# Dealing the row stores of the last two batches over six expert blocks

## What is computed

```python
logits = jnp.einsum('bsd,de->bse', x, gate_w)
top_vals, top_idx = jax.lax.top_k(logits, K)              # K = 2 of E = 8
gate_scores = jax.nn.softmax(top_vals, axis=-1)
...
h = jax.nn.silu(x @ w1 + b1) * (x @ w2 + b2)              # for each expert, 128 -> 256
expert_out = h @ w3 + b3                                  # 256 -> 128
return jnp.einsum('ebsd,bse->bsd', expert_out, w_dense)
```

## Time and profile before

| | us |
|---|---|
| median of 3 runs | 1115.79 (1115.34 to 1119.27) |
| profiled execution, its span | 1191.7 |

### The profile page before, as it was taken

How to read it: one execution, slowest core, us unless ns; L and a number is a source line. 1 busy time by engine, 2 the same in 40 slices (tenths; PEclk the granted TensorE clock), 3 DMA queues, 4 the chain that set the end, 5 groups by cost and what they waited for, 6 DMA issues and landing times. The chain is left out here.

```text
span 1191.7 us, 19302 instructions
## 1 busy us (share of the span) xinstructions
PE 993.4 (83%) x5725; PEld 373.4 (31%) x5725; DVE 912.5 (77%) x1983; ACT 816.4 (69%) x1555; POOL 664.7 (56%) x1061
## 2 busy tenths in 40 slices
PE   4699979898998989989999898888888865888780
PEld 2122222222222222222232222222145643655550
DVE  6788889987989989998998978998635734444667
ACT  2138888887877888877887777888756743565640
POOL 3833045565675656856667565364346556566562
PEclk9999999998989999999998989999689978999995
DMA  8758766664556656565555654332322433343456
GB/s 202 143 127 250 151 154 159 133 132 142 109 152 126 133 137 125 155 130 123 147 117 151 118 128 116 87 99 72 110 60 85 159 121 107 110 131 116 136 175 229
DMA packets 369049, 159.63 MB, mean 134 GB/s; under 512 B 290656, under 2 KB 333552, under 8 KB 365232
## 3 DMA queue, kind: packets, MB, share of 16 engines
q1 hardware_dynamic: 347376, 122.06, 44.7%
q0 software_dynamic: 9088, 18.76, 4.6%
q10 hardware_dynamic: 12480, 17.57, 4.2%
HBM read 87.85 MB, written 71.82 MB: 134 GB/s over the span
## 5 line engine op out<-in xcount | busy, mean ns | idle before, releaser
L1246 DVE TENSOR_REDUCE neg_max<-bank 128x1 f32<-128x512 f32 x1024 | 643.1, 680 | 86.9 <-PE bank L1979 73.9
L1755 ACT ACTIVATE probs<-bank 128x512 f32<-128x512 f32 x1024 | 545.3, 605 | 119.4 <-PE bank L1991 91.9
L1979 PE MATMUL bank<-Kt,Qt 48*128 48x512 bf16 x1024 | 348.4, 405 | 72.1 <-DVE neg_max L1246 51.9
L1991 PE MATMUL bank<-Qt,Kt 51*128 51x512 bf16 x1024 | 344.4, 401 | 13.4 <-ACT probs L1755 11.7
L2004 PE MATMUL bank<-probs,Vt 128*16 128x512 f32 x2048 | 283.6, 627 | 0.0
L1137 POOL DMA_INDIRECT y_dram<-y_rows,row_in x156 | 153.4, 983 | 99.6 <-DVE y_rows L1646 57.7
L1979 PEld LDWEIGHTS bank<-Kt,Qt 48*128 48x128 bf16 x1024 | 75.4, 94 | 418.5 <-DVE neg_max L1246 345.8
L1062 POOL DMA_INDIRECT rows_dram<-rows,slot x128 | 127.0, 992 | 45.5 <-issue 32.6
L1883 ACT ACTIVATE probs<-bank,w3b_cur 128x512 f32<-128x512 f32 x78 | 52.8, 687 | 99.0 <-PE bank L2080 45.4
L1639 DVE SCALAR_TENSOR_TENSOR probs<-bank,w3b_cur,probs 128x512 f32<-128x512 f32 x78 | 58.2, 748 | 69.8 <-ACT probs L1883 54.4
L2078 PE MATMUL bank<-ht_first,w_cur 128*128 128x512 f32 x156 | 71.1, 456 | 40.5 <-ACT w_cur L1869 24.5
(11 more groups left out here) (234 smaller groups left out, 1228.0 us busy)
## 6 DMA issues: line engine op xcount, KB each, us to landing
o_dram<-o_sb ACTq DMA_DIRECT2D x64, 256.0 KB, 3.0
row_in<-rows_dram SPq DMA_DIRECT2D x39, 260.0 KB
Qt<-q_dram SPq DMA_DIRECT2D x64, 128.0 KB
Kt<-k_dram SPq DMA_DIRECT2D x64, 128.0 KB
y_in<-y_dram SPq DMA_DIRECT2D x16, 512.0 KB
q_dram<-q_parts SPq DMA_DIRECT2D x48, 128.0 KB, 4.8
k_dram<-k_parts SPq DMA_DIRECT2D x48, 128.0 KB, 5.5
rows_dram<-rows SPq DMA_DIRECT2D x4, 1040.0 KB, 5.7
```

The source lines that it names most:

```text
L1246: dve.tensor_reduce(neg_max[:, side, a, col:col + 1], score_a[m % 3][:], AX_X, ALU.max, negate=True).then_inc(s_max, 1)
L1755: act.activation(probs[:, 4 * (j % 2) + (k ^ 1)], score_b[n % 3][:], ACT.Exp).then_inc(s_exp, 1)
L1979: pe.matmul(score_a[m % 3][:], Qt[b % BUFS][first:first + ROWS, n, P * c:P * c + P], Kt[b % BUFS][first:first + ROWS, n], start=True, stop ...
L1991: pe.matmul(score_b[m % 3][:], Kt[b % BUFS][first:first + ROWS + PARTS, n, P * c:P * c + P], Qt[b % BUFS][first:first + ROWS + PARTS, n], ...
```

## The change

The eight row stores of batch 14 no longer stand ahead of the y stores of block 9. They are issued behind the y stores of blocks 9, 10 and 11, three, three and two. Those of batch 15 move likewise from ahead of the y stores of block 12 to behind those of blocks 12, 13 and 14. `front_slots` stays where it is, in pieces 9 and 12. The stores themselves, their order among each other (k = 0 first) and their semaphores are the same.

```diff
+            def scatter_tile(f, i):
+
+                k, t = i // TT, i % TT
+                pool.indirect_dma_start(rows_dram, bass.IndirectOffsetOnAxis(ap=slot[:, k, t:t + 1], axis=0),
+                                        rows[:, f % 2, k, t], None).then_inc(s_scattered[f % 2], DMA)
+
...
-                    9: lambda: (front_slots(NB - 2), scatter(NB - 2, 0), scatter(NB - 2, 1)),
-                    12: lambda: (front_slots(NB - 1), scatter(NB - 1, 0), scatter(NB - 1, 1)),
+                    9: lambda: front_slots(NB - 2), 12: lambda: front_slots(NB - 1),
                 }
...
             for n in range(N_BLOCKS):
                 piece(n)
                 scatter_y(n)
+                if 9 <= n < 9 + 6:
+                    f, part = NB - 2 + (n - 9) // 3, (n - 9) % 3
+                    for i in range(3 * part, min(3 * part + 3, 2 * TT)):
+                        scatter_tile(f, i)
```

## The result

The changed kernel takes 1128.72 us (median of 4 runs, 1123.37 to 1130.09), beside 1115.57 us (median of 4, 1106.44 to 1119.27) for the kernel before on the same chip. The ratio is 1.0114, interval 1.0086 to 1.0142: 12.7 us slower (9.6 to 15.8), where I had forecast 8.5 us. The plain medians differ by 13.2 us; I go by the ratio.

The account below looks back on a forecast made before the run. The end was taken to hang on when row_load(19) may issue, with POOL's indirect DMAs ahead of it. 0 for step 1 and 8.5 us for steps 2 and 3, on 1115.8, gave 1124.3 us; range 1112 to 1131.

Parts of the forecast that it names:

- Step 3: Batch 15's row stores end behind block 14's y stores, not ahead of block 12's: turn(19) 6.7 to 11.9 us later.
- Step 2: POOL waits for batch 14's last row store to land before writing batch 15's slots: 1.8 us, bounds 0 and 5.1.
- Step 1: Y stores of blocks 9 to 11 issue 10.1, 6.3 and 2.5 us earlier, which buys nothing: cost 0, gain 0.
- Was PE there in time to notice?: PE reaches turn(19) at about 987 us, ahead of 1003 old and 1015 new, so the whole difference shows.
- runs dry: POOL idles for some us behind block 15's y stores, since weigh(16) stands behind turn(19) on DVE.
- The rival of late signals: Unexplained waits after finished matmuls and stretched SP copies rule the timed runs too: 0 to +3.7 us, chance 0.22.
- The rival of a dissolved stall: Eight row stores in one run cause the expert stage's stall and dealing ends it: 7 us faster, chance 0.12.
- The rival of slow trips: PE trips of about 8 us make turn(19) late anyway and hide the moved wait: +2.0 us, chance 0.06.
- The idle copies: In the old kernel, SP's eight unstretched copies make turn(19) due at 20.8 us, against 21.7 through block 12's y stores.

Follow-up runs that it names:

- e0: The kernel before, unchanged, profiled a second time: span 1117.1 us, own time 1118.87 us.
- e3: The kernel before with batch 15's eight row stores moved as one run to behind block 12's y stores: 1116.83 us, ratio 1.0003.
- e2: The changed kernel with only batch 14's row stores dealt out, batch 15's at once ahead of block 12's y stores as before: 1118.02 us, ratio 1.0021.
- e6: The changed kernel, unchanged, run in the longer condition beside the kernel before: median 1189.87 us, ratio 0.9987.
- e5: The changed kernel with a second slot tile for batch 15, against the kernel before in the longer condition: ratio 0.9977.
- e1: The changed kernel with only batch 15's row stores dealt out, batch 14's at once ahead of block 9's y stores as before: 1124.66 us, ratio 1.0081.

## Why the prediction was right, point by point

**Step 3, the mechanism, holds within 2 us.** Measured from the end of y11:

| | forecast | measured |
|---|---|---|
| old: turn(19) behind y11 | 21.7 | 959.61 - 939.47 = 20.1 |
| new: turn(19) behind its own y11 | 33.6 + 2.5 = 36.1 | 972.26 - 935.84 = 36.4 |

The end of the way was priced too high in both. From the end of the last store to turn(19) the prediction has 1.8 + 0.8 + 2.8 = 5.4 us; the traces have 4.2 us (e0, 955.45 to 959.61) and 4.9 us (changed, 967.39 to 972.26). The 1.8 us were read up to SP's load, so they held SP's own instructions already, and the 0.8 us count them again. The 0.7 us between the two traces are SP's: it waits for y12 at L664, the last step of row_load(19), but for R15 at L654, with the instructions of L661 still ahead of it. e3, which also ends with R15, has such a plus (0.9 us in the table).

**The size of step 3 was chosen too low.** Bounds were 11.9 us (1.27 us from DMA to DMA) and 6.7 us (0.96 us); I took 8.5, because the timed runs "leave less room for POOL than the trace shows". The runs showed the upper end. In both profiles of the 1115-us condition, whose spans are within 2 us of their own times, the spacing is 1.27 us. The changed kernel, timeline of POOL:
```profile
936.14 0.96 POOL L1062 DMA_INDIRECT rows_dram<-rows,slot  x1 [0.30 <-issue]
937.41 0.96 POOL L1062 DMA_INDIRECT rows_dram<-rows,slot  x1 [0.30 <-issue]
941.35 0.19 POOL L1051 CAST slot<-slot_f 128x8 uint32<-128x8 f32 x1 [2.98 <-DMA rows_dram<-rows,slot]
...
942.44 0.98 POOL L1143 DMA_INDIRECT y_dram<-y_rows,row_in  x1 [0.76 <-issue]
...
971.49 0.96 POOL L1143 DMA_INDIRECT y_dram<-y_rows,row_in  x1 [0.30 <-issue]
978.08 0.95 POOL L1143 DMA_INDIRECT y_dram<-y_rows,row_in  x1 [5.63 <-DVE y_rows L1655]
```
From 942.44 to 971.49 are 23 steps of 1.263 us. My reason for the lower value rested on a wrong split of the 75.9 us between span and median: I put it all down to the expert stage. By e0 that stage is 237.2 us (859.35 to 1096.5) where the first profile has 277.6: 40.4 us of the difference. Another 34.7 us lie ahead of it (weigh(0) at 894.06 against 859.35). At 237 us for 39 blocks there was room for POOL's 1.27 us. (A smaller slip: of POOL's slices in the earlier trace rows the 33rd is 5 tenths, not 6 as I wrote; nothing hangs on it.)

**Step 2 is there, and larger.** The pause ahead of the CAST was priced at 1.8 us; the third row above has 2.98 us, e2 has 2.83, and e2's whole time is +2.3 us. The 1.8 was read from the end of y11's last store to row_load(18), which was a short landing. How long a landing takes differs: behind the end of its store it is 1.3 us for y12 in e0 and for R15 in the changed kernel (2.22 and 2.27 us from the store's start in the chains above), but nearly 3 us for the last store of R14. Beside that one SP is issuing the idle copies (from 938.75 in the changed kernel, from 935.68 in e2); that these lengthen it is not shown. The Trainium skill, "DMA: Bandwidth & Descriptors", section "Anatomy of one DMA — SWDGE (gpsimd) path", gives about 2.0 us as the fixed cost of such a DMA, from its setup to its completion. Counted alike, from the start of the store, the chains here have 2.22 to 2.39 us, a little above it, and the wait ahead of the CAST 3.9 us (937.41 to 941.35), well above it.

**Step 1 is right: nothing waits for y9 to y11.** Its test was that weigh(13) to weigh(15) aren't released by y stores. In e0 they are at 938.75, 942.06 and 947.89 without such a wait, and of PE's 11.1 us of waits for loads from 911 to 962 us turn(19) has 9.6. e0, the turn ahead of it is not late at all:
```profile
944.41 0.66 PE L2065 MATMUL bank<-ident,row_in 128*128 128x128 f32 x4 [0.23 <-DMA row_in<-rows_dram]
```

**Steps 1 to 3 with measured terms.** With 1.27 us and a pause of 2.9 us the prediction's own sum is 11.9 - 1.8 + 2.9 = 13.0 us, and 13.7 us with the 0.7 us by which R15 is dearer to SP than y12; the traces have 13.8, the runs 12.7.

**"Was PE there in time to notice?" Yes.** PE's margin was put at 16 us (987 against 1003). In e0 it waits 9.59 us for turn(19) in the kernel before already, so nothing covered the delay, as the forecast needed. The margin is smaller than forecast, in part because the six trips from turn(12) to turn(18) (908.25 to 944.41) took 6.0 us each and not 5.4. POOL "runs dry" behind y15 too: 5.63 us in the last row above.

**The rival of late signals is true of a condition, not of this kernel.** It gave 0 to +3.7 us; e6 has -1.6 (-5.9 to +2.9). My error was to treat it as a question about the timed runs, with one answer. Its argument against (the 76 us) was right for the runs at 1115 us. That the change was measured in that condition was luck: the profile that I had was of the other one, where by e6 the forecast of a slower kernel would have failed.

**The rival of a dissolved stall fell**, but its test was badly put. I wrote that I'd be wrong if weigh(11) followed weigh(10) by less than 10 us. It does, 6.0 us (changed kernel, 918.54 to 924.59), and in e0 it does too, 6.0 us (919.65 to 925.68), without the change. The stall was the condition's, so its absence said nothing on the bunch. A test has to be one that the unchanged kernel would fail. e6 shows that dealing doesn't end the late signals either: 28.2 us of such waits with the stores dealt out.

**The rival of slow trips** needs trips of about 8 us; by e0 the mean is 237.2 / 39 = 6.1 us, and turn(19) stood waiting for its load. It has no support.

**The idle copies** did not come last: eight of them take 9.98 us in e0 and 10.83 us in the changed kernel, against 23.02 us in the earlier trace rows, so the 20.8 us that I gave them as unstretched stay ahead of y12's 21.7. This reading was right, and as close as forecast: 0.9 us between the two then, 1.1 us in e0.

**Open:** whether each four y stores ahead of the load cost 5.1 us by themselves, whether the second slot tile, which removes the pause in e5's trace, takes back 2.3 us, and whether larger rings would take away the 9.59 us that the kernel before still waits, all at 1115 us; why the landing ahead of the CAST takes longer than others, and what starts the late signals.

## What to carry to other kernels

Where a load waits for all stores of a kind, its start is set by the last of them. If that load is what the stage waits for and the storing engine issues without a pause, as here, then what is dealt between the stores on that engine is added to the wait in full: count the instructions between the first and the last store, each at its start-to-start time rather than its busy time, up to the last one. Bringing work forward on a queue pays only if someone waits for it, so ask of both ends of a swap who waits there. And where the profile's span is far from the median, compare stage by stage before it is decided which terms of the profile still hold.

## What the runs showed of the hardware

**A longer condition of a one-core program.** The kernel before, 19302 instructions on a single core, takes 1115 us in some groups of runs and 1190 us in others. It isn't only in the expert stage. The windows of 100 to 800 us (attention), two kernels: busy us of PE, of its weight loads, of DVE, ACT and POOL, each with its number of instructions, then the granted clock, the DMA share and GB/s. In e0:
```profile
100.00:800.00 700.00, 634.12 (x4360) 180.24 (x4352) 648.54 (x1353) 596.53 (x1190) 418.53 (x780) 1.00 0.60 138
```
in e6, the longer condition:
```profile
100.00:800.00 700.00, 622.32 (x4126) 173.29 (x4118) 617.64 (x1277) 566.05 (x1127) 401.89 (x738) 0.96 0.59 134
```
PE gets through 5% fewer instructions in the same 700 us, and the granted clock is 0.96 against 1.00. In the expert stage it is seen as waits of 7 to 12 us of ACT and PE that no row explains, 28.2 us of ACT's in 115 us of e6, none in e0. Most of POOL's DMAs keep their 0.96 us in both. That the clock and the waits have one cause is not shown. In one of e6's waits the clock falls late and not ahead of it: from 965 to 969 us PE is busy for 0.04 us at a granted clock of 1.00, and from 969 to 973 us the granted clock is 0.63 on average.

**An indirect store is dearer than its busy time.** In the stretch where the two batches are stored it is 0.95 to 0.98 us busy with 0.30 us of issue between two: 1.263 us from start to start over 24 in a row (942.44 to 971.49), also when row stores and y stores alternate. In e0, e2 and the changed kernel one y store each takes 1.38 us (935.57, 931.40 and 934.46), and at the end of e0's stage several take 1.01 to 1.15 us (from 1088.57 on); I don't know why.

**A landing has no fixed length.** From the start of an indirect store to its landing it is 2.22, 2.27, 2.28 and 2.39 us in the chains of e0, the changed kernel, e1 and e3. The store's own 0.96 us are inside that, so the landing is 1.3 to 1.4 us behind its end. Where POOL itself waited for its last store, it stood idle for 2.83 (e2) and 2.98 us (changed kernel) behind that store's end.
